# Two moves in the instruction order of an attention stage: where a head pair's prepared products stand, and where a unit's output product stands

## The reference, cut to what matters

```python
q_mid = rmsnorm(hidden_states @ q_a_w.T, q_a_ln_w)                       # [1024, 192]
q = (q_mid @ q_b_w.T).reshape(b, s, H, D_Q)                              # 16 heads of 128 + 64
k_pe = (hidden_states @ kv_a_w.T)[..., KVR:].reshape(b, s, H, D_ROPE)    # 64 per head
kv = rmsnorm(kv_lora, kv_a_ln_w) @ kv_b_w.T                              # latent of 64
q_pe, k_pe = apply_rope(q_pe, cos, sin), apply_rope(k_pe, cos, sin)
scores = einsum('bhqd,bhkd->bhqk', [q_nope, q_pe], [k_nope, k_pe]) * D_Q ** -0.5
ctx = einsum('bhqk,bhkd->bhqd', softmax(scores), v)
main_out = ctx.reshape(b, s, H * D_V) @ o_w.T
```

## Time and profile before

| what | value |
|---|---|
| median of 3 runs | 1306.22 us (1299.85 to 1313.52) |
| the profiled execution, its own time | 1304.03 us |
| its span, first to last instruction | 1302.2 us |
| mean granted TensorE clock | 0.961 |
| busy over the span: PE, PE weight loads, DVE | 91%, 64%, 68% |
| busy over the span: ACT, POOL | 50%, 41% |
| this stage (units 1 to 31) in the span | about 280 to 765 us |

### The profile page before, as it was taken

The page is one execution under the profiler, slowest core; times in us unless marked ns, Lnnn a source line. Parts: engine busy times, 40 slices in busy tenths (PEclk is TensorE's granted clock), DMA queues, the critical chain, the costliest instruction groups (busy, mean ns, idle before and its releaser), DMA issues.

```text
span 1302.2 us, 34623 instructions
## 1 busy us (share of the span) xinstructions
PE 1189.6 (91%) x14433; PEld 836.3 (64%) x14436; DVE 891.5 (68%) x1354; ACT 654.2 (50%) x1242; POOL 532.7 (41%) x531
## 2 busy tenths in 40 slices
PE   8999999997979898979797869999998998989997
PEld 5544334466767676767675657888853444678997
DVE  4689988367868687868675875645668673755555
ACT  3479978853434343434342424333245676435553
POOL 4257264327576666657575323544200000421221
PEclk8989999999989898989898978999999999989999
DMA  7780000011111111101010122010332410101110
GB/s 276 206 178 2 2 17 25 1 45 32 31 30 32 31 40 27 45 25 44 23 35 21 58 63 85 25 52 23 85 73 64 94 37 1 34 17 33 50 41 33
DMA packets 41699, 66.25 MB, mean 51 GB/s; under 512 B 8476, under 2 KB 27676, under 8 KB 40604
## 3 DMA queue, kind: packets, MB, share of 16 engines
q1 hardware_dynamic: 41544, 64.04, 17.8%
HBM read 45.60 MB, written 8.45 MB: 42 GB/s over the span
## 4 chain that ended last, share of the span: by engine, by line
PE 61%; DVE 12%; POOL 12%; issue 4%; ACT 4%; SPq 3%; DMA 3%; POOLq 0%; ACTq 0%; DVEq 0%
PE bank L1478 8%; PE bank L2148 6%; PE bank L2149 6%; PE bank L2150 6%; PE bank L1435 4%; PE bank L1938 4%; POOL qk0l L1676 3%; PE bank L1834 3%; PE bank L1298 3%; PE bank L1569 2%; PE bank L1972 2%; PE bank L1836 2%; PE bank L1835 2%; PE bank L1415 2%; DVE mpc L1377 2%
## 5 line engine op out<-in xcount | busy, mean ns | idle before, releaser
L1843 DVE TENSOR_REDUCE nmq<-bank 128x1 f32<-128x1024 f32 x128 | 155.1, 1212 | 95.8 <-PE bank L1836 94.3
L1858 ACT ACTIVATE P<-bank,nmq 128x1024 f32<-128x1024 f32 x128 | 142.8, 1115 | 144.6 <-DVE nmq L1843 143.8
L1456 ACT ACTIVATE Pb<-bank 128x512 f32<-128x512 f32 (+3 forms) x355 | 180.7, 573 | 31.6 <-PE bank L1435 10.9
L1306 DVE TENSOR_REDUCE mp<-bank 128x2 f32<-128x1024 f32 x128 | 153.5, 1222 | 29.7 <-PE bank L1298 28.9
L1834 PE MATMUL bank<-qk1h,qk0h 128*128 128x512 f32 x256 | 113.3, 443 | 46.7 <-POOL qk0l L1676 39.8
L1871 DVE STREAM_TRANSPOSE PT<-P 128x1024 f32<-128x1024 f32 x124 | 151.8, 1224 | 0.9 <-ACT P L1858 0.9
L1938 PE MATMUL bank<-PT,kv 32*64 32x128 f32 x7936 | 137.0, 275 | 7.9 <-issue 7.8
L1938 PEld LDWEIGHTS bank<-PT,kv 32*64 32x64 f32 x7936 | 118.5, 130 | 34.0 <-issue 33.8
L1377 DVE TENSOR_REDUCE mpc<-bank 128x2 f32<-128x1024 f32 (+2 forms) x96 | 88.3, 953 | 44.4 <-PE bank L1365 22.0
L1478 PE MATMUL bank<-Pb,vx 128*17 128x256 f32 (+3 forms) x1222 | 107.1, 411 | 0.7 <-ACT OTa L1492 0.5
L1836 PE MATMUL bank<-qk1h,qk0l 128*128 128x512 f32 x256 | 104.4, 408 | 0.7 <-issue 0.7
(11 more groups left out here) (354 smaller groups left out, 2912.9 us busy)
## 6 DMA issues: line engine op xcount, KB each, us to landing
t<-t SPq DMA_DIRECT2D x128, 64.0 KB, 2.4
wr<-wf SPq DMA_DIRECT2D x25, 256.0 KB, 2.7
wraw<-wf SPq DMA_DIRECT2D x8, 768.0 KB, 4.4
scratch<-stgr SPq DMA_DIRECT2D x4, 1024.0 KB, 4.0
Rs<-shares SPq DMA_DIRECT2D x64, 64.0 KB, 2.8
scratch<-stg SPq DMA_DIRECT2D x8, 384.0 KB, 2.6
qst<-scratch SPq DMA_DIRECT2D x9, 256.0 KB, 7.6
owT<-owT SPq DMA_DIRECT2D x1, 2048.0 KB, 11.5
```

Source lines behind the costliest of these rows:

```text
L1306: e.tensor_reduce(mp[:, w % 3, :, j, kh], wide[slot][:], AX, ALU.max).then_inc(ring_ok, 1)
L1456: e.activation(PBR[l][i % len(PBR[l])][:, 0:c], bank[b][:, 0:c], ACT.Exp, scale=0.25).then_inc(exp_ok[0], 1)
L1843: e.tensor_reduce(nmq[:, n % 8:n % 8 + 1], scores(u, i), AX, ALU.max, negate=True).then_inc(mp_ok, 1)
L1858: e.activation(probabilities(u, i)[:], scores(u, i), ACT.Exp, bias=nmq[:, n % 8:n % 8 + 1], accum_out=sums[:, u % 2, i:i + 1]).then_inc(ex ...
```

## The change

Two things change in `main_order()`. First, `PREP_AT` becomes a table with a row for each pair. For pairs 2 to 7 the products k = 0 to 5 move from the places 5, 8, 9, 12, 16, 17 to 1, 5, 9, 12, 13, 16; for pair 1 from the same to 5, 8, 9, 12, 13, 16. Second, project and add of unit u-2 move from behind score tile 0 of unit u to behind its score tile 1 (not in unit 31).

```diff
-PREP_AT = (5, 8, 9, 12, 16, 17)
+PREP_AT = ((5, 8, 9, 12, 13, 16),) + ((1, 5, 9, 12, 13, 16),) * 6
...
-    preps = {16 * (p - 1) + at: (p, i) for p in range(1, 8) for i, at in enumerate(PREP_AT)}
+    preps = {16 * (p - 1) + at: (p, i) for p in range(1, 8) for i, at in enumerate(PREP_AT[p - 1])}
...
     for u in range(1, 32):
         order.append(("score", u, 0))
-        output(u - 2)
+        if u == 31:
+            output(u - 2)
         prep(4 * u, "prep")
...
         order.append(("score", u, 1))
+        if u < 31:
+            output(u - 2)
         prep(4 * u + 1, "prep")
```

## The result

| kernel | median us | runs | ratio to the kernel before |
|---|---|---|---|
| before | 1309.87 | 4 (1299.85 to 1314.93) | |
| changed | 1262.39 | 4 (1260.25 to 1263.23) | 0.9644 [0.958, 0.9709] |

The change makes the program 3.6% faster. The forecast was 1262.4 us, and the measured median is the same to a tenth. Some of that is luck: single runs of the kernel before lie 15 us apart, a fourth run has moved its median from 1306.22 to 1309.87 us, and so the medians lie 47.5 us apart where 43.8 were forecast, while the two traces lie 40.8 us apart. The profiled execution of the changed kernel took 1263.23 us, its span is 1261.4, 40.8 us less than the span of before.

A forecast was written before the change was run, and what follows sets the result against it. PE was taken to bound the kernel, standing for POOL's late last differences at the head of pairs. Terms -45.0 + 3.0 + 0 - 1.8 = -43.8 us took the median from 1306.2 to 1262.4 us, range 1250 to 1282.

The forecast's parts named there:

- The six waits at units 8 to 28: PE's waits for POOL's last differences before tile 0 vanish, 35.95 us, plus 9.0 us of slow clock: -45.0 us.
- The step through SP, POOL and Q0: R2's rows land about 428.3, Q0 is done at 439.1, PE is free at 442.19: 3.1 us of slack.
- slow starts: Behind waits for POOL, PE runs at 1.2 GHz from tile 0 to tile 1; removing six saves 6 x 1.50 = 9.0 us.
- One sign of being wrong: The prediction would be wrong if POOL still stood for the swap of R2 beyond 4 us.
- the first who needs them is unit 14: R3, swapped in unit 11, is done some 7 us into unit 12, Q1 4 us later, before unit 14 needs them.
- The sentence that all copies find POOL done: ACT's copies wait for POOL two products back, and all of these are done by then.
- The output product behind tile 1: In twelve units PE waits for the exponentials before tile 1, 0.25 us later in each: +3.0 us.
- Units 29 and 30: No prepared product covers the addition ahead of `pv`; unit 29 at -0.5, unit 30 at +0.5: 0, between -2 and +2.
- Pair 1: The wait at unit 4 stays in kind; R3 moves into unit 3, POOL's chain starts 0.6 us earlier: -1.8 us.
- PE's pauses: Rival: PE's own pauses amid `pv`, 7.8 us before, grow; twice as many give 1271, three times 1279 us; chance 0.08.
- The rival that a part of the waits stays: R2's rows land later than counted, using up the slack; 5 us late gives 1274 us; chance 0.05.
- The rival of the exchange: Moving project and add behind tile 1 costs more in each of 27 units, `pv` waiting for the addition: 1324 us; chance 0.03.

The follow-up runs named there:

- four extra products: Changed kernel with four idle products (5.7 us in all) on POOL ahead of Q0 in pairs 2 to 7: 1286.19 us.
- R2 alone: Against the kernel before, pairs 2 to 7 at places 4, 5, 9, 12, 16, 17, project and add left behind tile 0: 1285.4 us.
- the places alone: Against the kernel before, only the new places of the prepared products; project and add stay behind score tile 0: 1261.78 us.
- the two kernels with R0 first: Changed kernel with pair 1 at 4, 5, 9, 12, 13, 16: 1258.56 us; the same with project and add behind tile 0 everywhere: 1252.53 us.
- no exchange in units 28 to 30: Changed kernel with project and add behind score tile 0 in units 28 to 31, behind tile 1 in all others: 1258.54 us.
- R0 in pair 1's first place: Changed kernel with pair 1's row at 4, 5, 9, 12, 13, 16, so R0 and R1 are swapped together in unit 1: 1258.56 us.
- second load later: Changed kernel with the load of the second expert's weights moved on SP's queue from unit 29's rec to unit 31's: 1268.14 us.
- POOL + 2 products: Changed kernel with two idle products (2.8 us in all) on POOL ahead of Q0 in pairs 2 to 7: 1265.94 us.

## Why the prediction was right, and where it was not

**The six waits at units 8 to 28.** Right in mechanism and size. The step through SP, POOL and Q0 gave a slack of 3.1 us; four extra products measured 2.8 to 3.0, and what the step left out is the 0.4 us from POOL's end to PE's start. Waits and slow starts together were to bring 7.5 us a pair less 0.5 for the exchange, 7.0; a pair became 61.3 - 54.5 = 6.8 us shorter, or 62.3 - 55.4 = 6.9 with its pauses. R2's rows were the last to come, 12.9 us behind the start of unit 10 where 13.2 were worked out, and from unit 5 to unit 28 PE stood for OTm only in units 4p and 4p + 3.

One sign of being wrong came up all the same: POOL was not to stand for the swap of R2 beyond 4 us, and it stood 5.26, 4.71, 6.33, 6.70, 3.87 and 4.93 us in the six pairs. The sign was badly chosen. POOL comes to R2 earlier now and so stands longer for rows that land when they were expected to; what decides is when Q0 ends.

**What was treated as a detail.** R3 and Q1 were followed only as far as "the first who needs them is unit 14". They are needed earlier by something else: ACT's copy of R1 cannot start before Q1 has left the staging tile. With R2 alone moved, a pair was 2.8 us longer than in the changed kernel, 2.2 of them such waits. The sentence that all copies find POOL done was right for the changed kernel, but about a half of the gain hangs on it.

**The output product behind tile 1, +3.0 us.** Right in sign and about right in size in the pairs: twelve waits for ACT of some 0.5 us where they were expected, 0.4 us a pair against the places alone and 0.9 between the two kernels with R0 first, where 0.5 was worked out. All of these are single traces.

**Units 29 and 30, "0, between -2 and +2".** This is the term that was mis-sized, twice over. Set against the kernel before, the tail should have lost the slow start of unit 28 (2.3 us) and the product of R3, which now stands in unit 27 (1.2 us), and kept the rest: 3.5 us shorter. Without the exchange it lost 6.5 to 7.4 us, since PE's wait for ACT in unit 29, which POOL had held up, shrank from 3.97 to 1.25 us (no exchange in units 28 to 30) and took its slow clock along. With the exchange it lost nothing: the wait for the addition was foreseen in place (I had `pv` slip by 3 us and found 2.3), but not that PE would run on at 1.2 GHz behind it, nor the longer pause. Against the kernels without the exchange there the tail is 7 to 8 us longer in the traces; 1.1 to 2.2 us of that are the pause, which may not be the exchange's doing.

**Pair 1, -1.8 us.** About right. Tile 0 of unit 4 came 1.5 us earlier, counted from unit 1, where 0.6 was worked out (the other 1.2 of the 1.8 are R3's product, which has moved ahead of that tile), and the wait fell from 3.85 to 2.76 us. The slow start stayed: 4.19 us from tile 0 to tile 1 of unit 4 against 5.11 before is the output product that has left this place, 0.9 us in every unit of this kind. One trace does not size this term to a us: the run without the exchange in units 28 to 30 has the same code up to unit 27, took 46.1 us from unit 1 to unit 4 where the changed kernel took 44.3, and waited 4.18 us.

**The sum.** Sorted into the stretches of the table above, the prediction had -0.6 us from unit 1 to 4 (1.8 less, and R3's product more), -5.8 to unit 8 (its wait of 6.28, +0.5 for the exchange), -33.9 to unit 28 (29.7 of waits, 6.7 of slow starts, +2.5) and -3.5 in the tail. The traces have -1.5, -4.2, -34.7 and +0.7. The tail came out 4.2 us worse and units 4 to 8 1.6 us worse, of which 0.8 are pauses of PE; the other two were 0.8 and 0.9 us better. So the stage gained 39.7 us in the traces and not 43.8, and unchanged code ahead of it and behind it moved by -2.8 and +1.7 us from one execution to the other. That the median met the forecast to a tenth is not precision; the six waits, less the exchange in their pairs, are 42 of the 44 us, and these were right.

**The rivals.** PE's pauses did not grow in the pairs of the two main traces: 5.4 us before and 4.3 after between units 8 and 28. That is no proof that they cannot: the other nine traces have 3.8 to 10.6 us there under that name, and the places alone, where PE has no wait for POOL beyond 0.67 us at units 8 to 28, have the most. No run shows what these pauses are. The rival that a part of the waits stays is what two idle products on POOL begin to show. The rival of the exchange had the right place, the addition behind the second maximum, but it decided only where a unit has no prepared product behind tile 1, 3 units and not 27; in ordinary units of the changed kernel PE stood for the addition once, 0.19 us.

## What to carry to other kernels

When an engine with time to spare stops the busiest one at regular places, spread its inputs over the interval; but follow every buffer it shares, since a product that is started earlier can hold up the copy two steps on, and the wait then appears under another engine's name. A reordering that helps while something else is late can cost more than it brings once that is cured, so try each half again after the other; here the kernel without the exchange, and with R0 of pair 1 earlier, had the lowest median, 1252.5 us, at the price of almost no slack in some pairs. And look at the last few iterations apart from the steady ones: work that covered a wait in the middle is missing there.

## What the runs showed of the hardware

PE pauses for no semaphore at fixed places of its instruction list. The same `pv` in unit 2, three matmuls before its end, paused for 0.95 us in the kernel before, 1.41 in the changed one and 0.91 to 1.75 us over all eleven traces. The longest such pause in the stage is 3.57 us (R0 in pair 1's first place). One of 2.75 us went on for its last 2 us while the DMA engines stood at a share of 0.02 or less (second load later).

The length of a wait alone does not tell whether the granted clock falls behind it. It was 0.55 in the 2 us behind a wait of 2.31 us (changed kernel) and 0.63 behind one of 2.45 us (R2 alone, 464.67), where `pv` took 3.10 us instead of 2.10; behind one of 2.37 us in the same trace (586.94) it stayed at 1.00, and so it did behind 2.08 us (POOL + 2 products, 684.17).

A wait that the trace calls "issue" can be a semaphore wait whose releaser ended just before: all waits of PE for the addition ended 0.1 us behind it and have that name. POOL's 5.99 us ahead of 671.04 in the changed kernel, beside PE's long pause, are called so too, and the weights that it waits for landed at 670.91. The code tells which.
